# Aggregation, edge and node stages of a graph network: sums over 128 nodes, a ring of four gather buffers, bias added outside PSUM

## The reference

```python
x = x + gnn0(layernorm(x))   # two graph convolutions
x = x + ffn0(layernorm(x))   # 6 experts, top 2
x = x + gnn1(layernorm(x))   # messages over edges
x = x + ffn1(layernorm(x))   # 8 experts, top 2

def graph_conv(x, W, b):     # in gnn0: to 128, relu, back to 256
    msgs = (x @ W)[src] * edge_weight[:, None]
    return segment_sum(msgs, dst) + b

def gnn1(v):                 # mish(x) = x * tanh(softplus(x))
    h = mish(v @ W_dense.T + b_dense)
    y = mish(edge_features @ W_edge.T + b_edge)
    rst = h + segment_sum(relu(h[src] + y), dst)
    return mish(rst @ W_out.T + b_out)
```

## Time and profile before

| | us |
|---|---|
| median of 3 runs (5725.0 to 5741.83) | 5736.12 |
| profiled execution, span | 6977.8 |
| PE / weight loads busy | 4133.3 / 3120.9 |
| DVE / ACT / POOL busy | 2046.0 / 1510.4 / 2925.0 |

### The profile page before, as it was taken

The page is one execution under the profiler, slowest core; times in us unless marked ns, Lnnn a source line. Parts: engine busy times, 40 slices in busy tenths (PEclk is TensorE's granted clock), DMA queues, the critical chain, the costliest instruction groups (busy, mean ns, idle before and its releaser), DMA issues. The chain is left out here.

```text
span 6977.8 us, 63984 instructions
## 1 busy us (share of the span) xinstructions
PE 4133.3 (59%) x16404; PEld 3120.9 (45%) x16404; DVE 2046.0 (29%) x4123; ACT 1510.4 (22%) x1776; POOL 2925.0 (42%) x3015
## 2 busy tenths in 40 slices
PE   3676666676567666666532962655555555616990
PEld 2444444444344444434322851455555554415780
DVE  4223222222222222222441334332222323421212
ACT  1223222223223222222210101311111112301110
POOL 0555554453455554454114013166666664041005
PEclk8666666666666666666566985655555555558995
DMA  2344443343233333233203222254554553013213
GB/s 93 119 130 134 131 132 124 120 135 115 94 104 112 102 102 104 95 98 103 52 23 111 82 84 60 68 162 155 161 162 159 160 165 101 1 60 116 66 59 112
DMA packets 347713, 744.50 MB, mean 107 GB/s; under 512 B 68177, under 2 KB 196313, under 8 KB 347538
## 3 DMA queue, kind: packets, MB, share of 16 engines
q1 hardware_dynamic: 161522, 392.68, 16.4%
q0 software_dynamic: 118176, 284.72, 14.2%
q10 hardware_dynamic: 67968, 66.60, 3.0%
HBM read 521.40 MB, written 222.32 MB: 107 GB/s over the span
## 5 line engine op out<-in xcount | busy, mean ns | idle before, releaser
L565 PE MATMUL conv_pz<-conv_we,conv_edge 128*128 128x256 f32 x3360 | 1394.5, 536 | 505.5 <-issue 500.4
L446 POOL DMA_INDIRECT conv_gath<-support_table,conv_idx x840 | 811.8, 966 | 890.0 <-POOLq L55 631.2
L1410 POOL DMA_INDIRECT x_node<-node_table,x_idx x840 | 874.0, 1040 | 711.5 <-POOLq L55 460.1
L446 POOL DMA_INDIRECT conv_gath<-hidden_table,conv_idx x840 | 807.2, 961 | 868.3 <-POOLq L55 619.5
L565 PEld LDWEIGHTS conv_pz<-conv_we,conv_edge 128*128 128x128 f32 x3360 | 794.9, 258 | 795.9 <-issue 677.2
L1425 PE MATMUL x_pa<-x_hot,x_node 128*128 128x64 f32 x3360 | 755.4, 422 | 627.5 <-PEq L55 377.0
L1425 PEld LDWEIGHTS x_pa<-x_hot,x_node 128*128 128x128 f32 x3360 | 729.1, 331 | 654.1 <-issue 654.1
L556 PE MATMUL conv_ps<-conv_hot,conv_gath 128*128 128x64 f32 x3360 | 588.2, 331 | 497.4 <-issue 200.6
L556 PEld LDWEIGHTS conv_ps<-conv_hot,conv_gath 128*128 128x128 f32 x3360 | 538.3, 243 | 537.8 <-issue 412.1
L1206 ACT ACTIVATE conv_q<-conv_q 128x1024 f32<-128x1024 f32 x210 | 221.9, 1057 | 2218.0 <-ACTq L55 1919.6
L456 DVE TENSOR_SCALAR conv_q<-conv_pz 128x1024 f32<-128x1024 f32 x210 | 257.2, 1225 | 1463.2 <-DVEq L55 1214.2
(11 more groups left out here) (213 smaller groups left out, 4461.1 us busy)
## 6 DMA issues: line engine op xcount, KB each, us to landing
conv_edge<-in_edge_t SPq DMA_DIRECT2D x210, 512.0 KB
edge_mish_table<-conv_neg SPq DMA_DIRECT2D x210, 512.0 KB
x_neg<-edge_mish_table SPq DMA_DIRECT2D x210, 512.0 KB
e_rows<-expert_rows SPq DMA_DIRECT2D x114, 256.0 KB, 3.7
expert_outs<-e_outs ACTq DMA_DIRECT2D x114, 256.0 KB, 2.2
expert_rows<-conv_zeros ACTq DMA_DIRECT2D x35, 512.0 KB
expert_outs<-conv_zeros ACTq DMA_DIRECT2D x35, 512.0 KB
conv_gath<-support_table,conv_idx POOLq DMA_INDIRECT x840
```

The lines of the kernel that those rows point to most:

```text
L446: pool.indirect_dma_start(gath[s][:, j, :], None, table[:, :], bass.IndirectOffsetOnAxis(ap=idx[:, half, col:col + 1], axis=0),).then_inc( ...
L565: pe.matmul(ps_z[r][:, j, :], edge[r][:, m, j * P:(j + 1) * P], we[:, m, :], start=m == 0, stop=False)
L1410: pool.indirect_dma_start(node[s][:, j, :], None, c.t3[:, :], bass.IndirectOffsetOnAxis(ap=idx[:, half, col:col + 1], axis=0),).then_inc(g ...
```

## The change

- CG = 8, C = 832, SLOTS = 4 (so IT = 26), W = 128: groups of 8 chunks, one-hots and sums of 128 columns, 104 groups a loop.
- `stage_conv` and `stage_edges`: four gather buffers of 8 chunks each; DVE gives the indices of one buffer at a time, as soon as its own sum is added. In `stage_edges` `neg`, `hot` and PSUM have 2 buffers, and `neg` is given back right after the subtraction.
- Products: no bias matmul. DVE adds the bias (broadcast to 128 partitions) while it moves the product from PSUM to an SBUF tile `z`, and PSUM is free then; `min` and the last step of mish read `z` in SBUF.
- A product still has 4 chunks (ZG), one after each sum: 4 an iteration, 104 a loop.
- `stage_node_mish`: normalising and turning run one step ahead, and PE's order is product, turn, turn back.
- The zero fill has 640 rows an iteration instead of 512.

```diff
-C = 840
-CG = 4
+C = 832
+CG = 8
-SLOTS = 6
+SLOTS = 4
-W = 64
+ZG = 4
+W = 128
...
 # stage_conv, gpsimd
-                    for half in range(2):
-                        take(pool, idx_ready[half])
-                        for s in range(half * 3, half * 3 + 3):
...
+                    for s in range(SLOTS):
+                        take(pool, idx_ready[s])
+                        for j in range(CG):
+                            pool.indirect_dma_start(
+                                gath[s][:, j, :], None, table[:, :],
+                                bass.IndirectOffsetOnAxis(ap=idx[:, s, j:j + 1], axis=0),
+                            ).then_inc(gathered[s], 16)
 # stage_conv, vector
+            def prepare(i, s):
+                nc.vector.tensor_copy(idx[:, s, :], cols(c.src, i, s)).then_inc(idx_ready[s], 1)
+                over = lambda a: cols(a, i, s).unsqueeze(2).to_broadcast([P, CG, W])
+                link(dve, nc.vector.tensor_tensor(hot[s][:], c.iota[:].unsqueeze(1).to_broadcast([P, CG, W]), over(rel), ALU.is_equal), own)
+                nc.vector.tensor_tensor(hot[s][:], hot[s][:], over(c.weight), ALU.mult).then_inc(hot_ready[s], 1)
...
-                nc.vector.tensor_scalar(q[r][:], ps_z[r][:], ZMAX, None, ALU.min).then_inc(z_ready[r], 1)
+            def biased(r):
+                take(dve, pz_ready[r % 2])
+                dve.sem_inc(edge_free[r], 1)
+                take(dve, neg_out[r], 16)
+                link(dve, nc.vector.tensor_tensor(z[r][:], ps_z[r % 2][:], bias[:].unsqueeze(1).to_broadcast([P, ZG, D]), ALU.add), own)
+                dve.sem_inc(pz_free[r % 2], 1)
+                nc.vector.tensor_scalar(q[r % 2][:], z[r][:], ZMAX, None, ALU.min).then_inc(q_ready[r % 2], 1)
-                link(dve, nc.vector.scalar_tensor_tensor(neg[r][:], q[r][:], -1.0, ps_z[r][:], ALU.add, ALU.mult), neg_own)
+            def negated(r):
+                take(dve, factor_ready[r % 2])
+                nc.vector.scalar_tensor_tensor(z[r][:], q[r % 2][:], -1.0, z[r][:], ALU.add, ALU.mult).then_inc(neg_ready[r], 1)
             def step(i, first, final):
+                for s in range(SLOTS):
+                    add(i, s)
+                    if not final:
+                        prepare(i + 1, s)
+                    biased(s)
+                    if s or not first:
+                        negated((s - 1) % SLOTS)
...
 # stage_conv, tensor
-                    last = pe.matmul(ps_z[r][:, j, :], ones[:], parts[:], start=False, stop=True)
+                    for s in range(SLOTS):
+                        segment(k, i, s)
+                        product(s)
...
 # stage_node_mish, vector
+            def biased(h):
+                take(dve, py_ready[h])
+                link(dve, nc.vector.tensor_tensor(z[h][:], ps_y[h][:], bias[:].unsqueeze(1).to_broadcast([P, 2, D]), ALU.add), own)
+                dve.sem_inc(py_free[h], 1)
+                nc.vector.tensor_scalar(q[h][:], z[h][:], ZMAX, None, ALU.min).then_inc(q_ready[h], 1)
...
             def step(g, h, first, final):
                 if not final:
+                    take(dve, xn_free[h])
                     normalise(dve, nc, c, xn[h], g + 1, h, xn_ready[h])
+                biased(h)
...
 # stage_edges, vector: message and step
+                link(dve, nc.vector.tensor_tensor(node[s][:], node[s][:], neg[n][:], ALU.subtract), add_own)
+                dve.sem_inc(raw_ready, 1)
+                dve.sem_inc(neg_free[n], 1)
...
+                    if s == 0:
+                        add(i - 1, SLOTS - 1)
+                        indices(i, SLOTS - 1)
                     message(k, i, s)
+                    if s:
+                        add(i, s - 1)
+                        if not final:
+                            indices(i + 1, s - 1)
...
 # stage_node_out, vector: begin
-                nc.vector.tensor_scalar(q[n][:], ps_y[n][:], ZMAX, None, ALU.min).then_inc(z_ready[n], 1)
+                link(dve, nc.vector.tensor_tensor(z[n][:], ps_y[n][:], bias[:].unsqueeze(1).to_broadcast([P, TG, D]), ALU.add), own)
+                dve.sem_inc(py_free[n], 1)
+                nc.vector.tensor_scalar(q[n][:], z[n][:], ZMAX, None, ALU.min).then_inc(z_ready[n], 1)
```

More of the change, by code:

```diff
@@ L377, in stage_conv @@
         gath = [sb(f"gath{s}", [P, CG, HID]) for s in range(SLOTS)]
-        hot = [sb(f"hot{half}", [P, HALF_COLS, W]) for half in range(2)]
-        we = sb("we", [P, KD, D])
-        bias, parts, ones = bias_buffers(sb)
-        ln2 = sb("ln2", [P, 1])
-        edge = [sb(f"edge{r}", [P, KD, CG * P]) for r in range(MISH)]
-        q = [sb(f"q{r}", [P, CG, D]) for r in range(MISH)]
-        neg = [sb(f"neg{r}", [P, CG, D]) for r in range(MISH)]
-        ps = [pb(f"ps{n}", [P, W]) for n in range(2)]
@@ L386, in stage_conv @@
-        ps_z = [pb(f"pz{r}", [P, CG, D]) for r in range(MISH)]
+        hot = [sb(f"hot{s}", [P, CG, W]) for s in range(SLOTS)]
+        we, bias = sb("we", [P, KD, D]), sb("bias", [P, D])
+        edge = [sb(f"edge{r}", [P, KD, ZG * P]) for r in range(SLOTS)]
+        z = [sb(f"z{r}", [P, ZG, D]) for r in range(SLOTS)]
+        q = [sb(f"q{n}", [P, ZG, D]) for n in range(2)]
+        ln2 = sb("ln2", [P, 1])
+        ps = [pb(f"ps{n}", [P, 512]) for n in range(2)]
+        ps_z = [pb(f"pz{n}", [P, ZG, D]) for n in range(2)]
@@ L401, in stage_conv @@
+        own, act_own, w_in = sem("own"), sem("act_own"), sem("w_in")
         block = ctx.enter_context(nc.Block())
@@ L508, in _ @@
             link(dve, nc.vector.tensor_copy(window[:], c.base[:]), own)
+            for s in range(SLOTS):
+                nc.vector.memset(hot[s][:], 0.0)
+            link(dve, nc.vector.memset(sums, 0.0), own)
             dve.wait_ge(w_in, 32)
-            split_bias(dve, nc, c, bias, parts, own)
-            dve.sem_inc(parts_ready, 2)
+            if part == 0:
+                dve.sem_inc(filled, 32)
             with dve.Fori(0, load_passes(dve)) as k:
-                for half in range(2):
-                    indices(0, half)
-                    one_hots(0, half)
+                for s in range(SLOTS):
+                    prepare(0, s)
                 step(0, True, False)
@@ L555, in segment @@
                 for j in range(CG):
-                    last = pe.matmul(ps[s % 2][:], gath[s][:, j, :], hot[half][:, at + j, :], start=j == 0, stop=j == CG - 1)
+                    last = pe.matmul(ps[s % 2][:, 0:W], gath[s][:, j, :], hot[s][:, j, :], start=j == 0, stop=j == CG - 1)
                 last.then_inc(ps_ready[s % 2], 1)
@@ L1332, in turn_back, with product @@
                 transpose_half(nc, c, ps_u[h], rows[h]).then_inc(pu_ready[h], 1)
-            def step(h, first, final):
-                if not (final and h):
-                    turn(1 - h)
+            def product(h):
                 take(pe, xt_ready[h])
@@ L1341, in step @@
                     for k in range(KD):
[L1342 to L1343 removed]
+                        last = pe.matmul(ps_y[h][:, s, :], xt[h][:, k, s * P:(s + 1) * P], wd[:, k, :], start=k == 0, stop=k == KD - 1)
                 last.then_inc(py_ready[h], 1)
[L1345 to L1348 removed]
+            pe.wait_ge(w_in, 32)
             turn(0)
+            turn(1)
             for h in range(2):
[L1351 removed]
+                product(h)
+                turn(h)
             with pe.Fori(1, G - 1) as g:
                 for h in range(2):
[L1354 removed]
+                    product(h)
+                    turn(h)
+                    turn_back(h)
             for h in range(2):
[L1356 to L1358 removed]
+                product(h)
+                turn_back(h)
+            for h in range(2):
+                turn_back(h)
 def stage_edges(nc, c):
@@ L1389, in _ @@
         def _(sp):
-            for n in range(RING):
+            for n in range(2):
                 sp.sem_inc(neg_free[n], 1)
@@ L1466, in step @@
-                    if s == 3 and not final:
-                        indices(i + 1, 0)
+                    if s:
+                        add(i, s - 1)
+                        if not final:
+                            indices(i + 1, s - 1)
             nc.vector.tensor_copy(rel[:], c.dstrel[:])
             link(dve, nc.vector.tensor_copy(window[:], c.base[:]), add_own)
+            for n in range(2):
+                dve.sem_inc(sum_free[n], 1)
             with dve.Fori(0, load_passes(dve)) as k:
-                indices(0, 0)
@@ L1473, in _ @@
-                indices(0, 1)
+                for s in range(SLOTS):
+                    indices(0, s)
                 for s in range(SLOTS):
```

297 lines of the change are left out of this document (109 added, 188 removed).

## The result

The changed kernel takes **5874.38 us** (median of 4 runs, 5866.72 to 5884.22), the kernel before 5738.98 beside it (4 runs, 5725.0 to 5741.98): ratio 1.0241, 95% interval 1.0207 to 1.0276. Forecast: 5888 us, range 5560 to 6090. The profiled execution of after took 5866.72 us and its span is 5864.9, so this trace, unlike that of before, is of an execution like the others.

The account below looks back on a forecast made before the run. In the runs POOL's indirect gathers bind the three loops. 5736.1 - 30 (fewer gathers) - 9 (ring) + 206 + 60 (longer gathers) - 90 (node stages) + 15 (ends) = 5888 us, range 5560 to 6090.

Parts of the forecast that it names:

- POOL binds the loops in the runs: Two aggregation loops and edge loop: POOL gathers nearly without pause in the runs, 840 gathers of 1.25 us, 1050 us each.
- the slow issue on PE belongs to the profiled execution: Three loops: PE's slow issue, starving POOL for 1250.5 us, is in the profiled execution and not in the timed runs.
- Rival 1: Three loops: PE's slow issue is in the runs too, so the ring saves 417 us, giving 5471 us; chance 0.20.
- The ring: Index buffers of the three loops, given back one slot at a time: saves only what the runs wait, -9 us.
- Gathers: Three loops: fewer gathers -30 us; gathers lengthened by VectorE operations, +206 us in aggregation and +60 us in edges.
- Nearer the lower half: Edge loop's longer gathers: +60 us taken between +4 and +137, because gather and subtraction keep a fixed phase.
- The mechanism: Gathers in the three loops: VectorE operations with SBUF tiles lengthen them; one ended 0.82 us after a subtraction, taking 1.87 us.
- Node stages: stage_node_mish and stage_node_out: running ahead breaks the wait between PE and VectorE, -50 and -40, together -90 us.
- Ends: End of each of the three loops: last slot drained with 8 chunks instead of 4, +5 us each, +15 us.
- The splitting of the bias: Work around the loops: new memsets of the one-hots replace the splitting of the bias, 0 us.
- PE and VectorE at 0: Three loops: wider sums on PE and the bias added on VectorE stay hidden under POOL's gathers, 0 us each.
- the forecast's +152: Whole kernel: all terms together take the time from 5736.1 to 5888 us, 2.6% slower.

Follow-up runs that it names:

- experiment 2: Kernel before with only its six gather buffers given back one at a time in all three loops: slow issue 6350.25 us (0.9315), quick issue 5702.34 us (0.9952).
- run 5: Changed kernel with the constant iota in PSUM in the three loops, run twice, both slow issue: 6104.87 us (0.8954) and 6104.67 us (0.8936).
- run 6: Changed kernel with products kept in PSUM and bias added by matmul as before the change: 5825.42 us beside 5873.79 of the changed kernel.
- runs 7: Changed kernel with two useless additions of 512 columns a slot, SBUF inputs, in both aggregation loops: 5868.27 us, -6 beside the changed kernel.
- run 8: Changed kernel with the last step of mish moved directly behind the one-hots in the aggregation loops: 5836.65 us, ratio 1.0169 to the kernel before.
- run 9: Changed kernel with no VectorE operation on two SBUF input tiles left in the three loops: 5459.82 us, ratio 0.9517 to the kernel before.
- run 4: The changed kernel run again, unchanged, on a quick-issue chip: 5873.79 us beside 5745.0 of the kernel before, ratio 1.0242.

## Why the prediction was right, and where only its sum was

- **POOL binds the loops in the runs** ("I take this to be no accident"): right where the times were taken, and what it rests on, that the profiled span's extra time is the waiting of POOL in the three loops, is borne out by the rest of the program, which takes the same on both kinds of chip (experiment 2). But "the slow issue on PE belongs to the profiled execution" failed: it belongs to a chip. Rival 1, worth 0.20, is what happens on such a chip: the ring gives -451 us there, where the rival had -417, though the kernel before takes 6801 there and not 5736. That the changed kernel was timed where issue is quick, like the kernel before, was luck: where it is slow the same changes with iota in PSUM are 10.5% faster than before. Nor does each iteration of a long loop stall in the runs, by which rival 1 would have held there: with quick issue PE has no issue gap in the three loops.
- **The ring**, -9: measured -33. The 9 was the difference of two numbers of over 1000 us, 1250.5 and 1241.7, and could not be had more exactly from them.
- **Gathers**, -30 + 206 + 60 = +236: the loops of after are 313 us longer from first to last gather than those of the ring's run (3537.5 for 3224.2). This is the term that was sized worst. For after I had 127, 127 and some 160 us of excess, 414; the trace has 111, 112 and 198, 421: two errors that nearly cancel. For before I had 24, 24 and 100; the ring's run has 14, 14.5 and 53, and it isn't known how much of the difference is the ring's own and sits in its -33. So the price per us of operation was near in the sum for the new kernel, and too high for the old. "Nearer the lower half" for the edges was wrong: the subtraction and the compare each held a gather in nearly every slot, and +145 against the ring's run lies even over the upper bound of +137 (104 x 2.3 - 100 is 139), because the 100 for before was too high; the 198 alone is under the bound's 239. Nor does a price per us describe what happens: an operation's excess depends on what stands before it (runs 5 to 8).
- **The mechanism** (held until 0.82 us after an operation whose tiles are in SBUF): shown by run 9, by runs 5 and 6 for a part each, and by the 103 and 95 slots of run 8. What I lacked was the shadow (runs 7 and 8). The minimum from SBUF to SBUF was rightly among the operations that can hold.
- **Node stages**, -90: -109 on quick issue by the two traces; alone on slow issue -78 and -90 by the times and -105 and -107 by the traces. A half step takes 135 / 26 = 5.2 us, not 6. The lower limit that I gave, PE's busy time (-46 and -55), was none: in the ring's run PE is busy 165.5 of 203 us of stage_node_mish at a granted clock of 0.58, in after 84.2 of 135 at 0.88. Some of its instructions went with the bias, and those left took less time at the higher clock.
- **Ends**, +15: wrong in sign. What lies between and around the loops and the node stages is 35 us shorter than in the ring's run, 17 of it between the second loop's last gather and stage_node_mish. The splitting of the bias, which the prediction put at nothing, is a part of it: in the ring's trace it takes 7 of these 17 us (3260.97 to 3268.08), and run 6, whose edit brings it back in the aggregation stages, is 22 us longer outside the loops than run 4. The rest wasn't tried.
- **PE and VectorE at 0**: right. PE is busy 689 of 1165 us, and even at a clock of 0.68 in the edge loop POOL doesn't wait.

With the measured terms: -33 + 313 - 109 - 35 = +136, and the time rose by 135. The sum closes because its last term is what the other two leave of the two traces' difference. That the forecast's +152 came so near is luck in part: 77 us too little for the gathers, against 24, 19 and 50 too little gain elsewhere.

## What to carry to other kernels

When a stage is bound by POOL's indirect gathers, look at the VectorE operations beside them whose tiles are all in SBUF, and not at VectorE's busy time: with one input in PSUM a 2.29 us operation held no gather, and doing that everywhere gave 414 us. Operations that can't be moved belong back to back, since the second stands in the shadow of the first; but only if the second never has to wait for its input (run 8: none held in 103 slots, 94 in 95).

When a profiled execution is longer than the runs, find out whether it came from a chip like theirs before arguing from either. The same change is 2.4% slower where issue is quick, and with one small edit 10.5% faster than before where it is slow. What it takes there without that edit wasn't measured.

## What the hardware showed that was not expected

- Two kinds of chip, or of condition of one: the same program at 5735 to 5745 or 6801 to 6826 us, with gaps of mostly 0.4 to 2.4 us in PE's issue in the three loops on the second and none on the first. In run 5 they come in 12 and 13 of 24 iterations of the two aggregation loops, nearly every second one, with 15 to 27 us in each and none in the others. What makes them wasn't found.
- A held gather ends 0.82 us after the operation that holds it, whatever runs by then. The Trainium skill, "SBUF - State Buffer", section "Who interferes with whom", says that the one who issues first has the shared ports for its whole instruction. With VectorE first the traces agree (2.22 us beside the 2.29 us subtraction, 0.94 us with one input in PSUM).
- With the gather first they don't: in after, 278 operations with two SBUF inputs began over 0.15 us into a gather that ran its usual 0.94 us, and took no longer for it (1.21 to 1.23 us, the subtraction 2.29). Only close together does it show. In 100 of the 208 slots of the run with the additions a gather began 0.02 to 0.04 us after the last step and went through, and the operation took 1.28 us for 1.22; a gather that began 0.05 to 0.08 us after it (15 times) was held. One that went through:

```profile
599.30 1.28 DVE L481 SCALAR_TENSOR_TENSOR conv_z<-conv_q,conv_z 128x1024 f32<-128x1024 f32 x1 [0.26 <-DVEq L54]
599.32 0.95 POOL L443 DMA_INDIRECT conv_gath<-support_table,conv_idx  x1 [0.30 <-issue]
```
